# A two-layer graph attention kernel: masks shared between two engines, tables made jointly, row scores moved

## The reference

```
layer 0: e = leaky(x@a1 [:,None] + x@a2 [None,:]);   masked where adj == 0
         x1 = layernorm(x + softmax(e, axis=1) @ x)
layer 1: wh = x1 @ W
         e = leaky(wh@a_src [:,None] + wh@a_dst [None,:]); masked where adj == 0
         out = layernorm(x1 + softmax(e, axis=1) @ wh + bias)
leaky(v) = v if v > 0 else 0.01 v
```

## Time and profile before

| | us |
|---|---|
| median of 3 runs | 557.29 (555.57 to 563.96) |
| the profiled execution | 553.18 |
| its span, first to last instruction | 551.1 |
| busy: TensorE, its weight load, VectorE, ScalarE, GpSimd | 451.5, 418.6, 409.1, 397.2, 126.4 |
| mean granted TensorE clock | 0.909 of full |

### The profile page before, as it was taken

The page is one execution under the profiler, slowest core; times in us unless marked ns, Lnnn a source line. Parts: engine busy times, 40 slices in busy tenths (PEclk is TensorE's granted clock), DMA queues, the critical chain, the costliest instruction groups (busy, mean ns, idle before and its releaser), DMA issues.

```text
span 551.1 us, 11884 instructions
## 1 busy us (share of the span) xinstructions
PE 451.5 (82%) x4420; PEld 418.6 (76%) x4420; DVE 409.1 (74%) x720; ACT 397.2 (72%) x619; POOL 126.4 (23%) x76
## 2 busy tenths in 40 slices
PE   0799768789987869988889529949999999989891
PEld 0379658678886868878889419929999998989891
DVE  3499989888996976889894989327567484847564
ACT  0794169778887594888955539168989898998961
POOL 0033332535255281435433100000000101001010
PEclk9987879899988899898989658968999999999997
DMA  8997899999999897999942001100212202020200
GB/s 209 302 219 189 240 220 291 322 291 312 299 301 328 237 312 218 319 287 301 308 140 95 0 0 41 39 0 7 82 28 60 86 0 86 0 86 0 87 11 10
DMA packets 80427, 87.59 MB, mean 159 GB/s; under 512 B 7440, under 2 KB 76304, under 8 KB 80400
## 3 DMA queue, kind: packets, MB, share of 16 engines
q1 hardware_dynamic: 44704, 52.49, 33.2%
q10 hardware_dynamic: 35696, 34.74, 23.1%
HBM read 77.78 MB, written 9.44 MB: 158 GB/s over the span
## 4 chain that ended last, share of the span: by engine, by line
issue 47%; PE 35%; DVE 10%; DMA 3%; POOL 2%; ACTq 1%; ACT 1%; POOLq 0%; DVEq 0%
PE acc L410 32%; DMA stage<-in_adj 3%; POOL small L949 2%; DVE narrow L780 2%; DVE kept L711 1%; PE srow L319 1%; PE misc L393 1%; DVE kept L714 1%; DVE neg L804 1%; DVE xy_old L716 1%; DVE xy_old L715 1%; DVE xy_old L713 1%; PE flip L422 0%; ACT x1s L559 0%; DVE turned L792 0%
## 5 line engine op out<-in xcount | busy, mean ns | idle before, releaser
L544 ACT ACTIVATE neg<-srow,dcol 128x512 int8 (+1 forms) x512 | 353.5, 879 | 31.1 <-issue 24.3
L410 PE MATMUL acc<-xy_old,pos 128*128 128x195 bf16 x1024 | 202.2, 265 | 39.9 <-issue 34.1
L410 PE MATMUL acc<-xy_old,neg 128*128 128x195 bf16 x1024 | 202.0, 266 | 0.0
L410 PE MATMUL acc<-stage,pos 128*128 128x195 bf16 x1024 | 181.2, 250 | 15.6 <-issue 8.2
L410 PE MATMUL acc<-stage,neg 128*128 128x195 bf16 x1024 | 181.1, 251 | 0.0
L410 PEld LDWEIGHTS acc<-xy_old,pos 128*128 128x128 fp8e4 x1024 | 108.3, 106 | 50.6 <-issue 48.1
L410 PEld LDWEIGHTS acc<-stage,pos 128*128 128x128 fp8e4 x1024 | 101.8, 99 | 21.6 <-issue 21.3
L410 PEld LDWEIGHTS acc<-xy_old,neg 128*128 128x128 fp8e4 x1024 | 107.8, 105 | 1.8
L780 DVE TENSOR_SCALAR narrow<-stage 128x4096 uint8<-128x4096 int32 x32 | 88.7, 2772 | 20.7 <-DMA stage<-in_adj 19.8
L410 PEld LDWEIGHTS acc<-stage,neg 128*128 128x128 fp8e4 x1024 | 101.3, 99 | 0.3
L949 POOL TENSOR_TENSOR small<-small,minus_half 128x4 f32<-128x4 f32 x16 | 28.4, 1777 | 234.1 <-DVE small L854 234.1
(11 more groups left out here) (113 smaller groups left out, 296.0 us busy)
## 6 DMA issues: line engine op xcount, KB each, us to landing
stage<-in_adj SPq DMA_DIRECT2D x64, 512.0 KB, 8.5
stage<-in_adj ACTq DMA_DIRECT2D x64, 512.0 KB, 8.6
spill<-turned SPq DMA_DIRECT2D x16, 512.0 KB, 7.8
turned<-spill SPq DMA_DIRECT2D x16, 512.0 KB, 3.8
out<-x1s SPq DMA_DIRECT2D x8, 128.0 KB, 2.0
kept<-in_x SPq DMA_DIRECT2D x4, 128.0 KB, 3.8
kept<-in_x ACTq DMA_DIRECT2D x4, 128.0 KB, 4.9
xn<-in_x SPq DMA_DIRECT2D x1, 512.0 KB, 9.2
```

What stands on the lines that cost most here:

```text
L410: last = nc.tensor.matmul(acc[:, r, c * XW:(c + 1) * XW], masks[c][:, t // BYTES, t % BYTES, r * P:(r + 1) * P], xy[layer][:, g * GT + t, ...
L544: last = nc.scalar.activation(o[:, t // BYTES, t % BYTES, :], srow[:, bass.ds((s % 2) * 512, 512)], ACT.Sign, bias=dcol[:, layer, col:col ...
```

## The change

- **Positive masks.** In layer 0 GpSimd makes only the first half of each positive mask (512 words). VectorE makes the second half, by one scalar_tensor_tensor, (sign XOR 0x38383838) AND adjacency, ahead of its own AND, which then waits for it (`pos_half`).
- **GpSimd's order.** `positive(s+1, 3)` comes ahead of `residual(s)`.
- **Tables.** `split` does X and Y in the same five instructions, over twice the elements.
- **Start.** The first two blocks of x are loaded first, the rest behind granule 0's lower half; ScalarE issues its second granule's load after `signs(0, 0, 0)`; TensorE turns two groups of x and takes the maximum before the others; VectorE makes the tables of granule 0 before it converts granule 0.
- **Laps.** `project` and `copy_x1` come one step earlier, `copy_wh` before `normalize`, with a semaphore of its own for the first copy.
- **Between the layers.** `NEAR` is 16 tiles. The near maximum is taken inside the last lap. Near tables are made for two granules, far tables for two. `scores1` and `mean1` are cut up: six supers of scores before the near tables are done, the rest of both by the end of granule (1, 0, 0). `row_factors1` comes before `mask(1, 1, 0)`.

```diff
-    NEAR = TILES - GT
+    NEAR = TILES // 2
+    CODES = 0x38383838
@@ sync
-            load_rows(sp, 0)
+            load_rows(sp, slice(0, RB))
             load(sp, LOWER, 0, 0)
+            load_rows(sp, slice(RB, IB // 2))
             load(sp, LOWER, 0, 1)
@@ tensor, body0 and between the layers
                 if first:
                     source_vectors()
+                else:
+                    project(s - 1)
                 granule(0, s + 1, 1)
-                if not first:
-                    project(s - 1)
+                if last:
+                    pe.wait_ge(xT_ready, NS + s)
+                    turn_max(0)
+                    spread_max(0)
                 granule(0, s + 1, 2)
...
             project(NS - 2)
+            pe.wait_ge(wh_kept, NS)
+            scores1(NS // 2, NS - 2)
             turn_x1(NS - 1)
             project(NS - 1)
+            pe.wait_ge(xT_ready, 2 * NS)
+            mean1(0, 2)
             turn_max(1)
             spread_max(1)
-            for g in range(NG - 1):
+            mean1(2, NS - 2)
+            granule(1, 0, 0)
+            mean1(NS - 2, NS)
+            scores1(NS - 2, NS)
+            for g in range(1, NG):
                 granule(1, 0, g)
-            granule(1, 0, NG - 1)
-            mean1()
-            scores1(1)
             score_row(1, 2)
@@ scalar
             act.dma_start(idf[:, :], ident).then_inc(s_a, 16)
-            load_rows(act, 1)
-            for g in range(SLOTS):
-                load(act, UPPER, 0, g)
+            load(act, UPPER, 0, 0)
...
-                signs(0, 0, 0, range(0, GT // 2))
                 act.wait_ge(shift_ready, 1)
                 exps(0, slice(0, TILES), mcol[:, 2:3], mcol[:, 3:4], exp_ready)
-                signs(0, 0, 0, range(GT // 2, GT))
+                signs(0, 0, 0)
+                load(act, UPPER, 0, 1)
@@ vector
+            def split(layer, g, rest):
+                step(nc.vector.tensor_tensor(rest, wh[layer][:, t, :].unsqueeze(1).broadcast_to(shape),
+                                             wts[:, :, t].unsqueeze(3).broadcast_to(shape), ALU.mult))
+                step(nc.vector.tensor_copy(hi, rest))
+                step(nc.vector.tensor_tensor(rest, rest, hi, ALU.subtract))
+                step(nc.vector.tensor_copy(mid, rest))
+                return nc.vector.tensor_tensor(lo, rest, mid, ALU.subtract)
...
+                if layer == 0:
+                    half = slice(GW // 2, GW)
+                    nc.vector.scalar_tensor_tensor(words(pos[:, g, :])[:, half], c[:, half], CODES, a[:, half],
+                                                   ALU.bitwise_xor, ALU.bitwise_and).then_inc(pos_half, 1)
+                    dve.wait_ge(pos_half, k + 1)
                 nc.vector.tensor_tensor(c, c, a, ALU.bitwise_and).then_inc(neg_ready, 1)
...
             dots0()
-            to_bytes(0, 0)
             column_max0()
-            turn(0, 0)
             shift0()
             tables0(0)
+            to_bytes(0, 0)
+            turn(0, 0)
+            mask(0, 0, 0)
...
             near_tables(1)
             mask(1, 0, 0)
-            near_tables(2)
+            mask(1, 0, 1)
             far_columns(1)
             column_max(1)
             far_shift()
             rescale(0)
-            mask(1, 0, 1)
             rescale(1)
-            rescale(2)
-            mask(1, 0, 2)
             dve.wait_ge(far_exp, 2)
+            far_tables(2)
+            mask(1, 0, 2)
             far_tables(3)
             mask(1, 0, 3)
             dve.wait_ge(x1_kept, NS + 1)
+            row_factors1()
             mask(1, 1, 0)
-            row_factors1()
@@ gpsimd
+            positive(0, 3)
             with pool.Fori(0, NS - 1) as s:
-                positive(s, 3)
                 for g in range(NG - 1):
                     positive(s + 1, g)
                 inverse_std(0, s)
+                positive(s + 1, 3)
                 residual(s)
-            positive(NS - 1, 3)
```

More of the change, by code:

```diff
@@ L344, in mean0, with mean1 @@
                 last.then_inc(mean_ready, 1)
-            def mean1():
-                for s in range(NS):
+            def mean1(first, end):
+                for s in range(first, end):
                     last = nc.tensor.matmul(mean_psum.rearrange("p (t d) -> p t d", d=D), onesN[:, :],
-                                            wh1[:, s * BYTES:(s + 1) * BYTES, 0:D], start=s == 0, stop=s == NS - 1)
-                last.then_inc(mean_ready, 1)
+                                            wh1[:, s * BYTES:(s + 1) * BYTES, 0:D], start=s == 0, stop=s == NS - 1,
+                                            skip_group_check=True)
+                if end == NS:
+                    last.then_inc(mean_ready, 1)
             def scores0(half):
@@ L359, in scores0, with scores1 @@
                 last.then_inc(scores_psum, 1)
-            def scores1(half):
-                for s in range(half * NS // 2, (half + 1) * NS // 2):
+            def scores1(first, end):
+                part = first // (NS - 2)
+                for s in range(first, end):
                     for r in range(RB):
                         b = s * RB + r
-                        last = nc.tensor.matmul(s_psum1[half][:, row_at(s % (NS // 2), r)], xT[:, b * P:(b + 1) * P],
+                        last = nc.tensor.matmul(s_psum1[part][:, row_at(s - part * (NS - 2), r)], xT[:, b * P:(b + 1) * P],
                                                 v_src[:, :], start=True, stop=True)
@@ L370, in tables0 @@
                 pe.wait_ge(s_a, 32)
-                pe.wait_ge(s_x, 32)
-                for t in range(RB):
+                pe.wait_ge(s_x[0], 16)
+                for t in range(2):
                     turn_x(t)
+                turn_max0()
                 pe.wait_ge(arep_ready, 1)
@@ L578, in body0 @@
                 for g in range(1, NG):
+                    if g == NG - 1 and not first:
+                        copy_x1(s - 1)
                     signs(0, s + 1, g)
@@ L582, in body0 @@
                         copy_weights()
-                if not first:
-                    copy_x1(s - 1)
                 signs(0, s + 2, 0)
                 load_next(s + 2, 0)
-                normalize(0, s)
                 if not first:
                     copy_wh(s - 1)
+                normalize(0, s)
             tables0()
@@ L612, in _ @@
             signs(1, 0, 0)
+            signs(1, 0, 1, range(0, GT // 2))
             copy_x1(NS - 2)
+            signs(1, 0, 1, range(GT // 2, GT))
             copy_wh(NS - 2)
[L615 removed]
             normalize(0, NS - 1)
@@ L618, in _ @@
             copy_wh(NS - 1)
-            signs(1, 0, 1, range(GT // 2, GT))
             act.wait_ge(shift_ready, 4)
@@ L693, in row_factors1 @@
             def row_factors1():
-                dve.wait_ge(scores_psum, 4)
+                dve.wait_ge(scores_psum, 5)
                 step(nc.vector.tensor_tensor(drop[:, 0:1], minus_shift[:, 1, 1:2], minus_shift[:, 1, 0:1], ALU.subtract))
-                for half in range(2):
-                    n = slice(half * IB // 2, (half + 1) * IB // 2)
-                    last = nc.vector.tensor_scalar(scol[:, n], s_psum1[half], 1 - SLOPE, drop[:, 0:1], ALU.mult, ALU.add)
+                for part, n in enumerate((slice(0, 3 * IB // 4), slice(3 * IB // 4, IB))):
+                    last = nc.vector.tensor_scalar(scol[:, n], s_psum1[part], 1 - SLOPE, drop[:, 0:1], ALU.mult, ALU.add)
                 step(last)
@@ L887, in _ @@
                 tables0(g)
+                if g < NG - 1:
+                    mask(0, 0, g)
             row_factors0()
-            dve.wait_ge(s_x, 32)
+            for n in range(2):
+                dve.wait_ge(s_x[n], 16)
             for s in range(NS - 1):
                 body0(s)
-            far_columns(0)
+            near_shift()
             mask(0, NS - 1, NG - 1)
-            column_max(0)
-            near_shift()
             dve.wait_ge(exp_ready, 5)
@@ L957, in positive @@
                 pool.sem_inc(pool_turn, 1)
-                nc.gpsimd.tensor_tensor(pos[:, g, :].bitcast(U32), mask_at(s, g).bitcast(U32),
-                                        neg[:, g, :].bitcast(U32), ALU.subtract).then_inc(pos_ready, 1)
+                half = slice(0, GW // 2)
+                nc.gpsimd.tensor_tensor(pos[:, g, :].bitcast(U32)[:, half], mask_at(s, g).bitcast(U32)[:, half],
+                                        neg[:, g, :].bitcast(U32)[:, half], ALU.subtract).then_inc(pos_ready, 1)
             pool.sem_inc(x1_kept, 1)
```

74 lines of the change are left out of this document (34 added, 40 removed).

## The result

The changed kernel takes 511.56 us in the median of four runs (510.13 to 513.15), against 556.43 us (550.12 to 563.96) for the kernel before on the same chip: a ratio of 0.923 with a 95% interval of 0.9145 to 0.9314. The prediction was 512 us. The profiled execution took 511.4 us with a span of 509.3; the span of before was 551.1, so 41.8 us have to be found in it.

The account below looks back on a forecast made before the run. The bound was taken to change by stretch: VectorE's chain at the start, a latency loop in the laps just above the DMA limit, standstills between layers. 553.2 - 7.5 - 11.6 - 24 = 510.1, plus half of 4.1: 512 us, range 502 to 527.

Parts of the forecast that it names:

- Start: Up to the first `to_bytes` of super 1: reached at 60.3 us instead of 67.85, 7.5 us gained, bounds 4 and 9.
- The joint tables: VectorE's X and Y tables in five double-size steps: 0.8 us saved per granule; a rival of no saving, 520 us, chance 0.06.
- The added instruction: VectorE's half mask in layer 0: 0.69 us, 0.75 with its wait, 3.0 a lap; upper bound 1.22 us each.
- half rate: Rival: VectorE's new mask instruction costs 0.55 us more each, lap 30.8 us, total 520 us; chance 0.12.
- Laps: Six laps of layer 0: 29.9 us each, 179.4 instead of 191.0, 11.6 us gained, bounds 6 and 16.
- The latency loop: Layer 0 laps: granule 3's `positive`, late behind `residual`, delays a chain through all engines back to the next late `positive`.
- port shared: Rival: in the laps, GpSimd instructions hold VectorE's masks through their common port; seven laps +43 us, total 564 to 566; chance 0.02.
- Passage: Between the layers, to granule (1, 1, 0): earlier tables, TensorE work in idle time, no standstill; 24 us gained, bounds 15 and 27.
- The last 1 us: Granule (1, 1, 0) of layer 1 starts at a full clock: another 1 us, within the 24 between the layers.
- ScalarE becomes the bound behind the gap: Rival: between the layers TensorE waits for ScalarE's signs at each granule; gain there only 15 us, total 521; chance 0.10.
- Moves costed at nothing: `project`, `copy_x1` and `copy_wh` in the laps: 1.0, 1.7 and 0.35 us, hidden beside TensorE and ScalarE idle time.
- half of 4.1 us: Whole run: the earlier median lay 4.1 us over the profiled execution; half was added to 510.1, giving 512 us.

Follow-up runs that it names:

- experiment 8: Kernel before with only GpSimd's order changed, granule 3's positive mask ahead of `residual`, nothing split: 542.31 us, ratio 0.9862.
- experiment 2: Changed kernel with GpSimd's old order, `residual` ahead of granule 3's positive mask, the mask split kept: 537.28 us, ratio 0.9698.
- experiment 9: Kernel before with only layer 0's positive masks split between VectorE and GpSimd, old GpSimd order: 562.76 us, ratio 1.0246.
- experiment 1: Changed kernel with whole positive masks (1024 words) on GpSimd again, new order kept: 513.73 us, ratio 0.9256.
- experiment 4: Changed kernel with row scores, `mean1` and row factors back in their old, later places: 526.7 us, ratio 0.9503.
- experiment 5: Changed kernel loading only half the adjacency columns per transfer from the second super on, same instructions, output not the reference's: 502.57 us, ratio 0.9052.
- experiment 3: Changed kernel with X and Y tables made one after the other, ten steps instead of five: 516.95 us, ratio 0.9335.
- experiment 6: Changed kernel with VectorE's half of the positive mask made twice in layer 0: 524.26 us, ratio 0.9439.
- Experiment 7: Changed kernel with ScalarE's `normalize` behind the next super's first signs in layer 1: 506.41 us, ratio 0.9115.
- experiment 10: Changed kernel with layer 1's `normalize` behind the next super's first signs and the second granule's load issued ahead of the exponentials: 506.1 us, ratio 0.9196.

## Why the prediction was right, point by point

*Start (7.5 predicted, 7.1 measured).* Exponentials and tables were placed right: 18.1 predicted, 17.58 measured; the first conversion 23.4 against 22.77. The second, 28.7, came at 29.90, after the wait for the late load, which I had priced at up to 1 us; it is 1.51. The joint tables: 0.8 us a granule was predicted, from 1.24 and 0.70 a step; the rows say 1.242 and 0.704. Taking them apart cost 5.4 us in all, 3.9 of it here, about 1 for each of four granules, as far as two profiled starts can tell.

*The added instruction (0.69 us and 0.75 with its wait).* L818 takes 687 ns, and four more of them cost 2.9 us in a lap, where I had 3.0. The bound of 1.22 us, and the rival "half rate" (520), are refuted. The Trainium skill ("Vector Engine (DVE) Microarchitecture Reference", Points that are easy to get wrong) gives half throughput for this form with two SBUF sources that are not bf16; for 512 words that would be, as an estimate, 0.15 + 1.07 = 1.2 us, and the measured 0.687 decides against it. Reading L838 was enough to know: an instruction of the same class with a row in the trace of before beats a rule. The 784 ns mean of the `kept` form isn't the rate: single ones take 1.23 us when they start under GpSimd's instruction (188.37, beside `residual`), and others 0.69.

*Laps (11.6 predicted, 12.4 measured).* The latency loop was the cause, as read from the lock on the conversions and from TensorE's late start: experiment 8 alone gives 12.5, and undoing the order (experiment 2) takes 22.2 back. The stretch of the conversions, which I had taken for a part of it, isn't needed for a long lap and doesn't make one (experiments 8 and 9). The next limit was named right as the transfers, 29.35 us of the predicted 29.2 to 30.4, and VectorE's lap at 28.6 was 28.5. But the prediction tied the gain of the laps to both parts, and only one carried it. The split alone is a loss of 6 us in the laps; what it brings on top of the new order isn't shown: experiment 1 lacks it and takes 3.5 us more in the laps and 2.2 in the median, but experiment 8 lacks it too and has after's laps. The rival "port shared" has its mechanism confirmed (3.33 us for a half mask caught under a conversion, in experiment 2) and its point of decision too: it lives in the long laps, and these need `residual` ahead of `positive`. Since that was gone, it didn't come.

*Passage (24 predicted, 22.3 measured with the rest).* This is the part that was off, by errors that partly cancel. In before's clock (19.54 us to add to after's times, 258.83 less 239.29) near tables start at 295.6, 293.6 predicted. The near maximum `mcol` waits 1.56 us for TensorE, which I had placed in a free moment: the granule ahead of it ran 7.9 us at a granted clock of 0.68, where one takes 5.7. That wait stands on VectorE ahead of `moments`, so `normalize` is late too, at 293.7 where before had it at 291.1, and the exponentials stand behind it. The last `acc` is read until 303.3, 300.8 predicted; the far rescaling starts at 321.8 and ends at 324.0, where I had the tables ready at 320 to 321; granule (1, 0, 0) starts at 324.1, 2.9 us late. From there to granule (1, 1, 0) I had counted 28.0 us, and it took 26.2, mostly because the 1.4 us for a low clock didn't come: granule (1, 0, 0) ran at 1.00. So granule (1, 1, 0) is at 350.25, 349.2 predicted.

The last 1 us, for a full clock in granule (1, 1, 0), came and was lost again. In before this granule starts at the low clock (0.50); after's starts at 1.00, and after's seventh `normalize` of layer 1 comes 158.3 us behind its start where before's comes 160.0. These 1.7 us are lost in the last super. TensorE stands 2.5 us there for `read_acc` in both kernels; behind it the clock fell in after and not in before. By window, first after, then before:

```profile
475.40:478.40 3.00, 3.00 (x21) 2.74 (x20) 1.94 (x3) 3.00 (x5) 0.00 (x0) 0.50 0.02 5
```

```profile
518.70:521.70 3.00, 3.00 (x38) 3.00 (x36) 1.93 (x3) 3.00 (x5) 0.00 (x0) 1.00 0.03 5
```

The profiled executions of experiments 2, 4, 5 and 8 show this fall too, those of 1, 3, 6 and 9 don't, and it costs 1.6 us; so it isn't this change that brings it. It is why the rest of layer 1 took 178.59 us for 178.75.

Experiment 7 shows something else that I hadn't read in the stretch left "as it is": each super of layer 1 was held by ScalarE's wait for the inverse deviation, and taking that away was worth 5 us. The rival "ScalarE becomes the bound behind the gap" (521) didn't come: `read_acc(1, 0)` and TensorE meet at 328.9 to 330.7 with both engines busy.

*Moves costed at nothing.* `project`, `copy_x1` and `copy_wh` cost nothing that shows: experiment 8, which lacks them and the split, has the same six laps (178.45 against 178.58). No run takes them apart from the split.

*The median.* I put half of 4.1 us on the sum for the spread of before; the changed kernel spreads over 3 us, and its median is 0.2 above the profiled execution. The term was not needed. That 512 lies within 0.5 us of the median is partly luck: the parts gave 510.1 for an execution that took 511.4, with the passage 1.7 short and the laps 0.8 over, and the added 2 us covered the difference.

## What to carry to other kernels

Where every engine has idle time in a loop, look for the chain that goes once around all of them, and for the instruction in it that stands behind one that could wait in the same queue: changing the order of two GpSimd instructions gave 12 us in six laps, while halving the GpSimd mask gave little with the right order and a loss with the old one. Then find the next limit by two opposite experiments, one that takes the resource's load away and one that doubles it: here they bracketed the lap at 28.5 for VectorE and 29.35 for the transfers. Read the unchanged stretches too: a wait worth a further 5 us stood in one.

## What the runs showed of the hardware

The DMA share isn't the rate. In the start, by window, after:

```profile
20.00:24.00 4.00, 2.11 (x10) 1.77 (x11) 3.93 (x4) 3.73 (x7) 0.00 (x0) 1.00 1.14 208
```

The engines are as full as in the laps (1.14 against 1.10) at 208 GB/s instead of 318 to 325. Which transfers make this difference, those of x or the sources' layout, wasn't tried. It fits that the earlier issue in experiment 10 brought nothing in the time; it doesn't prove it.

The lock between VectorE and GpSimd holds whichever comes second. In after it is GpSimd's `residual` that takes 2.10 us under a conversion (186.95), where one that starts ahead of the conversion takes 0.73 (165.34 in experiment 2). VectorE's half mask beside it then takes 1.23 us instead of 0.69 (188.37), but a wait for the transfers follows (194.31), and nothing is seen to wait for `residual`. The lock was not removed by the change, but moved to an instruction off the loop.
